# The rows of the first eight tiles are normalised on GpSimd instead of DVE

## The reference

```
xn  = (x - mean(x)) / sqrt(var(x) + 1e-5)            # per row of 512
out = x + attention(xn) + fp8_product(xn)

attention, per head (16 heads of 128):
  q, lk = rope(rmsnorm(xn @ Wq + bq)), rope(rmsnorm(xn @ Wlk + blk));  lv = xn @ Wlv + blv
  entries = per group of 4 rows: softmax(xn @ Wcmp + bcmp) weighted sum of xn   # 256 rows
  ck, cv  = rope(rmsnorm(entries @ Wk + bk)), entries @ Wv + bv
  sparse  = softmax over the 8 largest of q @ ck.T (causal) times cv
  local   = softmax over this and the previous window of 128 keys, q @ lk.T, times lv
  out     = (sparse + local) * 0.5 @ Wo + bo
fp8_product: xn and a 512x512 matrix scaled, rounded to fp8, multiplied, scaled back
```

## Time and profile before

| | us |
|---|---|
| three runs | 2492.25, 2493.53, 2493.62 (median 2493.53) |
| span of the profiled execution | 2492.2 |
| busy PE / DVE / ACT / POOL | 2462.4 / 1996.7 / 1675.3 / 1749.7 |

### The profile page before, as it was taken

One profiled execution on the slowest core, in us unless ns is written; L12 is line 12 of the kernel. 1 busy time (PEld: TensorE's weight loads), 2 busy tenths in 40 slices (PEclk: granted clock), 3 DMA queues, 4 the chain that ended last, 5 costly groups with the idle time before them and its releaser, 6 DMA issues. The chain is left out here.

```text
span 2492.2 us, 56206 instructions
## 1 busy us (share of the span) xinstructions
PE 2462.4 (99%) x15574; PEld 2190.6 (88%) x15606; DVE 1996.7 (80%) x6637; ACT 1675.3 (67%) x4866; POOL 1749.7 (70%) x3150
## 2 busy tenths in 40 slices
PE   7999999999999999999999999999999999999998
PEld 6888888888888988888888889888888888888887
DVE  7788888888778887787777888887878878888786
ACT  5667777767666677667666666767676666666665
POOL 6787787776786666666677766666667767676674
PEclk9999999999999999999999999999999999999999
DMA  5433233333332122121441221221235213212301
GB/s 159 136 107 113 71 109 115 117 109 117 123 119 82 52 90 90 60 90 43 151 150 53 81 82 60 90 86 64 78 124 166 94 59 100 75 61 94 98 10 52
DMA packets 183530, 232.36 MB, mean 93 GB/s; under 512 B 19762, under 2 KB 101172, under 8 KB 183220
## 3 DMA queue, kind: packets, MB, share of 16 engines
q1 hardware_dynamic: 182644, 228.50, 28.3%
q10 hardware_dynamic: 576, 0.26, 0.1%
HBM read 162.64 MB, written 65.01 MB: 91 GB/s over the span
## 5 line engine op out<-in xcount | busy, mean ns | idle before, releaser
L1598 POOL TENSOR_TENSOR t<-raw,tB 128x128 f32<-128x128 f32 x512 | 226.4, 464 | 593.8 <-DVE raw L1167 593.7
L987 ACT ACTIVATE ch<-bVC,blT 128x128 fp32r<-128x128 f32 x512 | 160.5, 365 | 511.1 <-PE bVC L726 511.1
L631 PE MATMUL bQK<-wh,xh 128*128 128x512 f32 x1024 | 424.4, 414 | 0.0
L632 PE MATMUL bQK<-wl,xh 128*128 128x512 f32 x1024 | 403.8, 394 | 0.0
L633 PE MATMUL bQK<-wh,xl 128*128 128x512 f32 x1024 | 401.4, 392 | 0.0
L1542 POOL TENSOR_TENSOR r<-ss,mh 128x4 f32<-128x4 f32 x256 | 286.4, 1119 | 60.1 <-DVE ss L1175 57.5
L647 PE MATMUL bVC<-wh,xh 128*128 128x256 f32 x1024 | 310.0, 303 | 0.0
L954 ACT ACTIVATE P<-P,nm,r 128x256 f32<-128x256 f32 (+1 forms) x512 | 295.3, 583 | 0.0
L1203 DVE CUSTOM_DVE_ANT_0 P<-bS,cst 128x256 f32<-128x256 f32 (+1 forms) x512 | 204.2, 399 | 110.5 <-PE bS L679 106.1
L649 PE MATMUL bVC<-wh,xl 128*128 128x256 f32 x1024 | 289.4, 283 | 0.0
L648 PE MATMUL bVC<-wl,xh 128*128 128x256 f32 x1024 | 289.0, 282 | 0.0
(11 more groups left out here) (188 smaller groups left out, 7617.9 us busy)
## 6 DMA issues: line engine op xcount, KB each, us to landing
wh<-kept SPq DMA_DIRECT2D x144, 256.0 KB, 4.1
wl<-kept SPq DMA_DIRECT2D x144, 256.0 KB, 4.6
kept<-wh SPq DMA_DIRECT2D x48, 256.0 KB, 3.2
kept<-wl SPq DMA_DIRECT2D x48, 256.0 KB, 3.4
woh<-kepto SPq DMA_DIRECT2D x48, 256.0 KB, 3.2
wol<-kepto SPq DMA_DIRECT2D x48, 256.0 KB, 3.7
ini<-in_hidden_states SPq DMA_DIRECT2D x24, 256.0 KB, 4.5
xs<-xsh SPq DMA_DIRECT2D x24, 256.0 KB, 2.5
```

The source lines that it names most:

```text
L631: e.matmul(bQK[:, :], a, b, start=kt == 0, stop=False)
L632: e.matmul(bQK[:, :], a, bl, start=False, stop=False)
L1598: last = e.tensor_tensor(t2[:, :, :, d_], raw[:, u % 2, :, :, s_], tB[:, :, u % 8, d_].unsqueeze(1).broadcast_to([128, 2, 2, 32]), ALU.mult)
```

## The change

For the first eight tiles L1288's operation is issued on POOL, directly behind the power of the tile, by a new function `first_rows`. It carries the waits on the loaded rows, on the power (`rstd`) and, from tile 4 on, on the free slot of `xt` (`et`). On DVE `normalise` keeps, for these tiles, the wait on `xn` and the operation L1294. It concerns steps -8 to -1 on POOL, so that `first_rows(t)` is queued ahead of the weight chunk that is split at the same step.

```diff
@@ -1282,10 +1282,10 @@
 
             def normalise(t):
                 xs = xt[:, t % XR, :]
-                e.wait_ge(S["rstd"], t + 1)
-                if t >= XR:
+                if t >= FIRST_TILES:
+                    e.wait_ge(S["rstd"], t + 1)
                     e.wait_ge(S["et"], t - XR + 1)
-                e.tensor_scalar(xs, rows(t), st[:, t % 2, 6:7], st[:, t % 2, 9:10], ALU.subtract, ALU.mult).then_inc(S["xn"], 1)
+                    e.tensor_scalar(xs, rows(t), st[:, t % 2, 6:7], st[:, t % 2, 9:10], ALU.subtract, ALU.mult).then_inc(S["xn"], 1)
                 e.wait_ge(S["xn"], t + 1)
                 if t >= 2:
                     e.wait_ge(S["ew"], t - 1)
@@ -1545,6 +1545,14 @@
                 e.wait_ge(S["xv"], t + 1)
                 e.tensor_tensor(st[:, t % 2, 9:10], st[:, t % 2, 8:9], mh[:, 0:1], ALU.pow).then_inc(S["rstd"], 1)
 
+            def first_rows(t):
+                rows_loaded(e, t)
+                e.wait_ge(S["rstd"], t + 1)
+                if t >= XR:
+                    e.wait_ge(S["et"], t - XR + 1)
+                e.tensor_scalar(xt[:, t % XR, :], rows(t), st[:, t % 2, 6:7], st[:, t % 2, 9:10], ALU.subtract,
+                                ALU.mult).then_inc(S["xn"], 1)
+
             def power_ck(k):
                 e.wait_ge(S["cke"], k + 1)
                 e.tensor_tensor(sm[:, 14:15], sm[:, 13:14], mh[:, 0:1], ALU.pow).then_inc(S["ckp"], 1)
@@ -1687,6 +1695,7 @@
                     power_ck(block_at(s, "rope"))
                 if s < 0 and tile_at(s, "power") is not None:
                     power_x(tile_at(s, "power"))
+                    first_rows(tile_at(s, "power"))
                 if s < 0:
                     for q, c in enumerate(CHUNKS):
                         if c[0] == "w" and c[3] == s:
```

## The result

Before 2493.53 us (median of 5 runs, 2492.25 to 2494.30), after 2502.76 us (5 runs, 2502.09 to 2503.12): 9.2 us slower, ratio 1.0037 with a 95% interval of 1.0026 to 1.0049. My forecast was 2492.5, with a range up to 2494.8. (The runs lie 1.8 us above their own spans, in after 2503.12 over 2501.3, not the 1.3 that I took from a median and the span of one execution.)

What follows compares the result with a forecast made beforehand. PE was taken to bound the span, DVE and ACT's bT turn the prologue; a 1.1 us earlier unit 0, cut to 1.0 by POOL, gave 2491.2 us span, plus 1.3 for a 2492.5 us median, range 2490.9 to 2494.8.

Steps and rivals of the forecast that it cites:

- the turn of 3.75 us: Prologue, one turn through bank bT from `lo_x` to `lo_x`: stays 3.75 us though DVE can save 0.54 per tile.
- DVE's list is now 3.2 us long: Tiles 2 to 5: with DVE's list at 3.2 us, the late turn of 4.30 us shrinks by some 0.5.
- What it adds: Eight 128x512 two-pointer scalings on POOL: 0.65 us each plus 0.09 wait, 0.74 per tile, 5.9 us in all.
- POOL falls behind: Rival at `power_ck(0)`: starting later than 40.4 loses the gain; at 1.01 per scaling 2494.7 us; chance 0.22.
- one of the signs that I had named for being wrong: Sign of error: `raw` of unit 0 after 42.0 with DVE idle before L1395 for POOL.
- POOL's side: Prologue on POOL: later splits and added rows make `power_ck(0)` start at 39.4 instead of 38.54; gain of 1.0 left.
- 3.6 us against the turn of 3.75: POOL's prologue step: power 0.57, rows 0.74 and split 2.29 us make 3.6, which barely fits the turn.
- rows of 3.0 us less the 1.1: Tiles 1 to 4 on POOL: after the chunk 4 wait absorbs 1.1 us, its split slips 0.9, 23.51 to 24.4.
- slip by 1.0 us: SP's queue: second split ends 1.0 us later, so chunk 3 and all behind it are issued 1.0 later.
- PE's rate: Rival at unit 0's start: 1.1 us of unit 0 run at half rate, gain 0.5, 2493.0 us; chance 0.18.
- is not in it: Behind unit 0's `raw`: tile 7's L1288 is outside the chain; PE's 0.3 us there ends as waiting before 50.26.
- `rows(7)`: POOL's scaling of tile 7: takes POOL to 41.3, before unit 0's `raw` is there.

Runs made afterwards that it cites:

- the addition and the move: After with rows on POOL by adding the negated mean, and in SP's queue chunk 5 and small loads moved behind the parks of tiles 0 and 1: 2492.82 us.
- The run of the forms: After with a different form of the POOL scaling in each of the eight tiles; forms with subtract 1.93 to 2.07 us, without 0.69 to 0.76; no kernel time told.
- the cheap form: After with DVE negating the mean and POOL adding it and multiplying, instead of subtracting: 0.76 to 0.87 us per scaling; 2495.79 us without a change in SP's queue.
- the kernel with the addition: After with DVE negating the mean and POOL adding it and multiplying, SP's queue unchanged: 2495.79 us, ratio 1.0009.
- tile 0 alone on POOL: Before with only tile 0 normalised on POOL, by addition, and tile 1's power ahead of the first split (the run whose L1291 took 1.35): 2493.34 us, ratio 0.9998.
- the kernel with the unread scaling: Before, DVE normalising as before, with an extra subtract scaling on POOL behind each of the eight powers, its output never read: 2502.37 us, ratio 1.0036.
- after with the move in SP's queue: After (subtract form) with chunk 5 and small loads moved behind the parks of tiles 0 and 1 in SP's queue: 2501.73 us, ratio 1.0035.

## Why the prediction was wrong

**What bounds.** Right: the turn of 3.75 us. With the addition and the move it stayed at 3.73 to 3.78 up to tile 3, though L1288 had left DVE. Wrong: "DVE's list is now 3.2 us long". With POOL busier, L1294 took 1.09 us in each turn instead of 0.75 and the list behind it was stretched too; DVE was busy 9.38 of the 10 us from 20 to 30, for 9.61 before.

**What it adds.** Here it failed: "0.50 is the lower end and twice that, 1.01, the upper ... I take 0.65". The rows took 2.07 to 2.14 us, over three times the term and twice its upper end. I bounded the price by rows with the same shape (L1613) and with pointers, all of which multiply, and took for granted that another ALU operation costs the same. The run of the forms shows that `subtract` is worth 1.3 us of the 2.07, the second pointer 0.07. A bound by nearest rows has to ask for each property of the new instruction (shape, operands, operation) whether any row shares it; none of those had `subtract` in a tensor_scalar on POOL. The rival "POOL falls behind" had the right mechanism, and the wrong price: with 2.07 it is not `power_ck(0)` alone that is late but every step, 5.04 against 3.75. `power_ck(0)` came at 47.82 where I had 39.4, and `raw` of unit 0 at 49.51 where I had 41.0, with DVE idle before L1395 for POOL, one of the signs that I had named for being wrong.

**POOL's side.** With 2.07 put into it, "3.6 us against the turn of 3.75" becomes 5.04; tile 1's rows are then ready at 13.08 + 2.07 = 15.15, `lo_x(0)` at 15.15 + 1.11 + 0.15 = 16.4 (measured 16.43), and four turns of 5.04 later `lo_x(4)` at 36.6 (measured 36.65, before 31.00): the 5.6 us by which `ckv` is late. The method held, the term did not. One sentence of this part does not add up even so: rows of 3.0 us less the 1.1 that the wait for chunk 4 absorbs are 1.9, not 0.9. With the addition and the move that split began at 25.11, 1.6 later than the 23.51 of before.

**What I missed.** I let SP's queue slip by 1.0 us and followed it to chunk 4 only. The parks of the fp8 tiles stand behind it too, and ACT's cast of tile 4 waits for the first. With the cheap form this costs 3 us (2495.79 to 2492.82), more than the wait of 1.95 us itself; in its profile PE's faster level also came later. In after `lo_x(4)` is as late without it, so there POOL's pace hides it at least up to this point.

**PE's rate.** I gave it as a rival for the first half of unit 0. In after the level was reached by 43.04; it mattered in the kernel with the addition (products 0.43 us apart from 39.85) and behind PE's idle time at 56 us. What raises it is not settled here. It also differs from profile to profile: the eight products of `ckv` took 3.54 us before, 3.62 in after, 2.56 with tile 0 alone on POOL and 2.60 in the kernel with the unread scaling. A difference of up to 1 us in the start of unit 0 between two profiles can therefore be this and nothing else.

**The tail.** That L1288 of tile 7 "is not in it" was true, but its successor on POOL is: 49.15 to 51.20 ahead of `rope_b(0)`. I had seen `rows(7)` take POOL to 41.3, "before `raw` is there" (41.0 + 0.69 = 41.7). With 0.76 us per scaling it came close: in the kernel with addition and move `rope_b(0)` began at 42.28, right behind `raw` (41.51 + 0.69 = 42.2).

**The shared port pair.** The Trainium skill, "SBUF — State Buffer", section "SBUF: two separate sides", calls the port pair of GpSimd and VectorE an exclusive lock. That agrees with the rows: L1294 took 1.10 us beside each split and the split's second half 1.58 us instead of 1.27, so 0.3 us per step, as forecast. With tile 0 alone on POOL, L1291 (24.65 to 26.00) ended only behind the split's second half (24.45 to 25.72). This was the smaller part of the loss: the larger was the length of one operation, which none of the rows from before has.

## What to carry to other kernels

Before work is moved to another engine, time the very instruction there (operation, operands, shape) in one tile of the real kernel: eight forms fitted into one launch here and would have settled the price. A scaling with `subtract` on GpSimd took 2.07 us where `add` of the negated value took 0.76, so negate the small operand on the engine that makes it. And when a queue slips, follow it to its end: what was late was not the load behind the split but a store further back, on which a slot was waiting.

## What was not expected of the hardware

- On GpSimd a tensor_scalar 128x512 in float32 with `subtract` in first place took 1.93 to 2.07 us in the run of the forms, with `mult` or `add` as the second operation and by pointer or constant; with `mult` or `add` in first place 0.69 to 0.76. Beside DVE's work each was longer in places: 2.35 in the kernel with the unread scaling, 0.87 in the one with the addition. A tensor_tensor `subtract` of the same shape took 1.27 us, as `mult` did (1.26).
- Idle stretches of 1.13 and 1.28 us on PE were followed by a granted clock of 0.57 over 4 us in the profile of after. In the profile of after with the move in SP's queue, stretches of 1.06 and 1.28 us in the same places were followed by 1.00. With 16 and 13 small products there instead of 8 and 4 it was 1.00 too, with no gain in the median.
- The granted clock read 1.00 from 39 to 42 us in the kernel with the addition while products 128x512 stood 0.43 us apart, which is the slower level.
